# A Toeplitz and scan stage whose entries PE spreads into PSUM, with eight resident tiles selected late

## The reference, cut to what matters

```python
xn = (x - mu) / jnp.sqrt(var + LN_EPS) * ln_gamma + ln_beta   # x itself is layer-normed before
dA = jnp.exp(-jnp.exp(log_A) * dt[:, None]); dB = B_param * dt[:, None]
h = dA * h + dB * u[..., None]                                 # for each time step
y = einsum('dn,bdn->bd', C_param, h) + D_param * u
...
x = x + (residual + y @ W_out.T + b_out)
x = x + attention(ctx, ctx, layernorm(x)) @ W_out.T + b_out    # 64 keys, 16 heads
x = x + gated_ternary_ffn(layernorm(x))                        # 256 -> 1024 -> 1024 -> 1024 -> 256
```

## Time and profile before

| | |
|---|---|
| median of 3 runs | 933.9 us (932.27 to 935.5) |
| the profiled execution | 934.08 us, its span 932.3 us |
| PE busy | 869.6 us, 93% of the span |
| DVE, ACT, POOL busy | 514.6, 493.6, 183.2 us |
| chain that ended last | PE 89%, DVE 5%, issue 4%, ACT 1% |
| DMA | 61.79 MB; queue q8 for instructions: 24 packets, 0.39 MB |
| 20.0 to 51.4 us | PE busy 6.6, DVE 30.5, ACT 23.1, POOL 18.1; DMA share 0.96, 261 GB/s |
| 51.4 to 101.2 us | PE busy 44.1, DVE 36.9, ACT 28.7, POOL 36.4; granted clock 0.91 |
| 101.2 to 167.0 us | PE busy 58.3, DMA share 0.87 |

### The profile page before, as it was taken

One profiled execution on the slowest core, in us unless ns is written; L12 is line 12 of the kernel. 1 busy time (PEld: TensorE's weight loads), 2 busy tenths in 40 slices (PEclk: granted clock), 3 DMA queues, 4 the chain that ended last, 5 costly groups with the idle time before them and its releaser, 6 DMA issues.

```text
span 932.3 us, 15096 instructions
## 1 busy us (share of the span) xinstructions
PE 869.6 (93%) x5570; PEld 697.0 (75%) x5570; DVE 514.6 (55%) x927; ACT 493.6 (53%) x761; POOL 183.2 (20%) x201
## 2 busy tenths in 40 slices
PE   1168999899999999999999999999999999999997
PEld 0068867677777778777877887778778777777886
DVE  7987485465446464555555555554555456553411
ACT  2927533476356735764475536653575366635432
POOL 1567800500041002200230014000500050003000
PEclk9679999999999999999999999999999999999999
DMA  9961797500110002000200010001100110001000
GB/s 340 243 162 55 261 387 306 226 1 1 52 45 0 0 22 73 0 0 15 81 0 0 0 73 22 0 0 51 45 0 0 51 45 0 0 23 45 1 1 25
DMA packets 15497, 61.79 MB, mean 66 GB/s; under 512 B 2835, under 2 KB 4502, under 8 KB 14646
## 3 DMA queue, kind: packets, MB, share of 16 engines
q1 hardware_dynamic: 15430, 61.31, 19.0%
q0 software_dynamic: 32, 0.00, 0.0%
HBM read 49.63 MB, written 23.20 MB: 78 GB/s over the span
## 4 chain that ended last, share of the span: by engine, by line
PE 89%; DVE 5%; issue 4%; ACT 1%; POOL 0%; DMA 0%; SPq 0%; DVEq 0%; POOLq 0%
PE pair L1342 51%; PE pair L1329 11%; PE pair L1354 6%; PE pair L1269 4%; PE pair L1280 3%; PE pair L1296 3%; PE pair L470 2%; PE pair L477 2%; PE pair L1289 1%; PE pair L1319 1%; PE pair L1236 1%; PE pair L484 1%; PE pair L539 1%; DVE GG L337 1%; DVE stn L343 1%
## 5 line engine op out<-in xcount | busy, mean ns | idle before, releaser
L950 ACT ACTIVATE vbuf<-pair,scl 128x512 f32<-128x512 f32 x128 | 87.8, 686 | 231.0 <-PE pair L1342 222.1
L1342 PE MATMUL pair<-h2hi,h_turned 128*128 128x512 f32 x512 | 202.6, 396 | 0.0
L1342 PE MATMUL pair<-h2lo,h_turned 128*128 128x512 f32 x512 | 199.6, 390 | 0.0
L1342 PE MATMUL pair<-h1hi,h_turned 128*128 128x512 f32 x384 | 153.1, 399 | 0.0
L1342 PE MATMUL pair<-h1lo,h_turned 128*128 128x512 f32 x384 | 150.0, 391 | 0.0
L1118 DVE TENSOR_TENSOR h1lo<-vbuf,h1hi 128x512 fp32r<-128x512 f32 x80 | 57.7, 722 | 120.1 <-ACT h1hi L951 119.3
L1342 PEld LDWEIGHTS pair<-h2hi,h_turned 128*128 128x128 f32 x512 | 96.2, 188 | 25.2 <-issue 5.9
L1342 PEld LDWEIGHTS pair<-h2lo,h_turned 128*128 128x128 f32 x512 | 96.2, 188 | 19.3
L1118 DVE TENSOR_TENSOR h2lo<-vbuf,h2hi 128x512 fp32r<-128x512 f32 x64 | 44.2, 691 | 107.2 <-ACT h2hi L951 107.1
L1329 PE MATMUL pair<-zThi,w_turned 128*128 128x512 f32 x224 | 92.0, 411 | 2.9 <-DVE vbuf L1142 2.9
L1142 DVE SCALAR_TENSOR_TENSOR vbuf<-pair,scl,sg 128x512 f32<-128x512 f32 x64 | 47.9, 750 | 80.5 <-ACT sg L939 60.8
(11 more groups left out here) (145 smaller groups left out, 1593.3 us busy)
## 6 DMA issues: line engine op xcount, KB each, us to landing
h_turned<-d_h SPq DMA_DIRECT2D x2, 4096.0 KB, 15.1
xres<-in_x SPq DMA_DIRECT2D x8, 512.0 KB, 7.5
tok<-in_xs SPq DMA_DIRECT2D x8, 512.0 KB, 12.2
EE<-alpha_rows SPq DMA_DIRECT2D x16, 256.0 KB, 10.7
ring<-kernel_rows SPq DMA_DIRECT2D x16, 256.0 KB, 4.3
xr<-x_rows SPq DMA_DIRECT2D x8, 512.0 KB, 3.5
out<-xr SPq DMA_DIRECT2D x16, 256.0 KB, 2.1
x_rows<-xres SPq DMA_DIRECT2D x7, 512.0 KB, 12.4
```

The lines of the kernel that those rows point to most:

```text
L950: e.activation(vb[:, s % 2, :], h_ps[s % 4], ACT.Gelu, scale=sc)
L1342: ins = e.matmul(bank, w[:, k, m * P:(m + 1) * P], src[part][:, k, :], start=(k == 0 and part == 0), stop=(k == HC - 1 and part == 1))
```

## The change

It has these parts.

1. Entries. The store to `alpha_rows` and the sixteen entry loads are gone. PE spreads the exponents: for each channel a 64 x 64 matmul whose stationary operand is one column of the identity, broadcast to 64 columns, writes the exponent row to 64 partitions of PSUM. `spread_entries(n)` does groups n and n + 4 (64 matmuls), four times. ACT's `entry_exp` reads PSUM (`pair[STAGE[g]]`) and writes `EE`.
2. Row sums. All four column blocks accumulate in one PSUM pair with a shifted `pick` matrix in place of `ones`, so that two evacuations do instead of eight; the eight stores to DRAM remain. ACT's evacuation stands inside its norms, ahead of the fourth one (`ROWS_AT`).
3. Tiles. Eight resident Toeplitz tiles in place of the ring of four: four where the ring was, four where the weights w1 and w2 come later. All sixteen tile loads are issued at once in `sync_mixer`. All eight selects stand in `gpsimd_core`, after the third gamma.
4. Statistics. Eight of the 32 tile statistics (tiles 8 to 15) go from DVE to ACT (`tile_stats`: a Copy and a Square pass with summed output).
5. Small work. The D edits of `GG` and their undoing go from DVE to GpSimd and ACT; the PSUM clear of the state banks goes from DVE to five PE matmuls; ACT does 18 instead of 20 of each 32 norms; the loads of w1, w2, w3 to SBUF also wait for the last within.

```diff
+STAGE = {0: 3, 4: 0, 1: 2, 5: 1, 2: 3, 3: 2, 6: 0, 7: 3}
+EXP_AT = {g: n + 1 for n, g in enumerate(STAGE)}
-ACT_SHARE = 20
+ACT_SHARE = 18
+ACT_STATS = (8, 16)
+ROWS_AT = 3
+PAD = L
...
     def sync_mixer(e):
...
-        e.wait_ge(coef, 2)
-        for u in range(2):
-            e.dma_start(alS[P * (1 - u):P * (2 - u), :], al2[:, u, :]).then_inc(al_st, 16)
...
-        e.wait_ge(al_st, 32)
-        for g in range(2):
-            entries_load(e, g)
         e.dma_start(bo[:, :], a["ab"].partition_broadcast(P)).then_inc(wo_in, 16)
         e.dma_start(woT[:, :, :], a["aW"]).then_inc(wo_in, 16)
-        for v in range(4):
-            for h in range(2):
-                u = 2 * v + h
-                e.wait_ge(k_ev, u + 1)
-                c = (1 - h) * (P * L) + v * 2048
-                e.dma_start(kr[0, c:c + 2048].rearrange("(q m) -> q m", q=4), ksb[0:P:32, u, :]).then_inc(kr_st, 16)
-        for n in ("xW", "keys", "scl"):
-            e.dma_start(t[n], a[n]).then_inc(k_in, 16)
+        for h in range(2):
+            e.wait_ge(k_ev, h + 1)
+            for v in range(4):
+                c = (P * (1 - h) + 32 * v) * PAD
+                e.dma_start(kr[0, c:c + 32 * PAD].rearrange("(q c m) -> q c m", q=4, c=8)[:, :, 0:L],
+                            ksb[v:P:32, h, :].rearrange("q (c m) -> q c m", c=8)).then_inc(kr_st, 16)
         e.wait_ge(kr_st, 128)
         e.wait_ge(kr_pad, 16)
         for g in range(4):
             tt_load(e, g)
-        for g in range(2, NGRP):
-            entries_load(e, g)
+        for g in range(4, NGRP):
+            if g == 6:
+                e.wait_ge(nat_v, 1)
+            tt_load(e, g)
+        for n in ("xW", "keys", "scl"):
+            e.dma_start(t[n], a[n]).then_inc(k_in, 16)
 
     def sync_core(e):
-        for g in range(4, NGRP):
-            e.wait_ge(w_ps, 2 * (g - 4) + 2)
-            tt_load(e, g)
         e.wait_ge(h_ps, NOCT)
...
     def gpsimd_prep(e):
...
-        mask(e, 0)
...
-        for g in range(1, 4):
-            mask(e, g)
-        e.wait_ge(t_mask, 8)
 
     def gpsimd_core(e):
         e.wait_ge(wo_in, 32)
-        done = 0
-        for g, until in ((4, 0), (5, 0), (6, 0), (7, 4), (None, TILES)):
...
+        e.wait_ge(z_h, 3)
+        for g in range(NGRP):
+            mask(e, g)
+        e.wait_ge(t_mask, 2 * NGRP)
+        for tile in range(TILES):
+            bias(e, tile)
...
+        def tile_stats(first, until):
+            here, n = slice(first, until), until - ACT_STATS[0]
+            e.wait_ge(xr_in[first // 4], 16)
+            if n > 4:
+                e.wait_ge(t_var, n - 4)
+            for j in range(first, until):
+                e.activation(junk[j % 4], xres[:, j, :], ACT.Copy, accum_out=tsum[:, 0, j:j + 1]).then_inc(t_sum, 1)
+            e.wait_ge(t_sum, n)
+            e.activation(tsum[:, 1, here], tsum[:, 0, here], ACT.Copy, scale=-1.0 / (16 * DM)).then_inc(t_mean, 1)
+            e.activation(mvn[:, here, 0], tsum[:, 0, here], ACT.Copy, scale=1.0 / DM).then_inc(t_mean, 1)
+            e.wait_ge(t_mean, n // 2)
+            for j in range(first, until):
+                e.activation(junk[j % 4], xres[:, j, :], ACT.Square, bias=tsum[:, 1, j:j + 1], scale=1.0 / 16, accum_out=mvn[:, j, 1:2]).then_inc(t_var, 1)
...
+                if c == ROWS_AT:
+                    row_evac()
...
-        for v in range(4):
-            row_evac(v)
-        e.wait_ge(const, 9)
+        e.wait_ge(const, 10)
+        tile_stats(8, 12)
+        for g in (0, 4):
+            entry_exp(g)
+        tile_stats(12, 16)
+        for g in (1, 5, 2):
+            entry_exp(g)
         norm_apply(0)
-        entry_exp(0)
         norm_apply(1)
-        for g in range(1, 3):
+        for g in (3, 6, 7):
             entry_exp(g)
...
     def tensor(e):
...
         e.wait_ge(g_row, 7)
-        e.wait_ge(d_add, 4)
+        def spread_entries(n):
+            for i in range(GRP):
+                for g, h, u in ((n, 0, 0), (n + 4, 1, 1), (n, 1, 0), (n + 4, 0, 1)):
+                    rows, c = slice(N * u, N * u + N), GRP * g + i
+                    ins = e.matmul(pair[STAGE[g]][L * h:L * h + L, N * i:N * i + N], ident[rows, c:c + 1].to_broadcast([N, L]), al2[rows, 1 - h, :], start=True, stop=True)
+            ins.then_inc(e_ps, 1)
+        spread_entries(0)
+        e.wait_ge(pk_done, 7)
+        e.wait_ge(w_row, 2)
+        spread_entries(1)
+        e.wait_ge(e_rdy, EXP_AT[4])
+        spread_entries(2)
+        e.wait_ge(d_add, 2)
+        e.wait_ge(e_rdy, EXP_AT[5])
         for v in range(4):
...
-                    ins = e.matmul(kps[v % 2][h][32 * q:32 * q + 32, :], ones[N * h:N * h + N, 0:32], GGf[N * h:N * h + N, c:c + 8 * L], start=True, stop=True)
+                    ins = e.matmul(kps[h][32 * q:32 * q + 32, :], pick[N * h:N * h + N, 3 - v:35 - v], GGf[N * h:N * h + N, c:c + 8 * L], start=(v == 0), stop=(v == 3))
+        ins.then_inc(k_ps, 1)
+        e.wait_ge(e_rdy, EXP_AT[2])
+        spread_entries(3)
+        e.wait_ge(k_ev, 2)
+        e.wait_ge(dec0, 1)
+        e.wait_ge(z_b, 2)
+        for k in range(5):
+            e.matmul(hps[k % 2].rearrange("p (a d) -> p a d", a=4), ident[:, :], dec[:, :, 0].unsqueeze(1).to_broadcast([P, 4, P]), start=True, stop=True)
```

More of the change, by code:

```diff
@@ L79, in mixer_parts @@
     rev = sb("rev", [P, P], "c")
-    ones = sb("ones", [P, 32], "c")
+    pick = sb("pick", [P, 35], "c")
     stn = sb("stn", [P, TILES, 6], "d")
@@ L220, in gpsimd_prep @@
         e.memset(rev[:, :], 0.0).then_inc(const, 1)
-        e.memset(ones[:, :], 1.0).then_inc(const, 1)
+        e.memset(pick[:, :], 0.0).then_inc(const, 1)
         e.memset(mhalf[:, :], -0.5).then_inc(const, 1)
@@ L240, in gpsimd_prep @@
             e.tensor_tensor(rn[:, 0, here], sv[:, here], mhalf[:, 0:SB], ALU.pow).then_inc(powd, 1)
-        mask(e, 0)
-        e.wait_ge(t_mask, 2)
+        e.wait_ge(d_in, 32)
+        e.wait_ge(w_row, 2)
+        e.wait_ge(g_row, 7)
+        for row in (0, N):
+            v = GG[row:row + 1, :, L - 1]
+            e.tensor_tensor(v, v, edit[row:row + 1, 0, :], ALU.add).then_inc(d_add, 1)
+        e.wait_ge(d_add, 2)
+        power(0)
+        e.wait_ge(k_ps, 1)
+        e.wait_ge(powd, 1)
+        for row in (0, N):
+            e.tensor_copy(GG[row:row + 1, :, L - 1], edit[row:row + 1, 1, :]).then_inc(g_back, 1)
+        e.wait_ge(g_back, 2)
+        power(1)
         e.wait_ge(nat_v, 1)
+        e.wait_ge(powd, 2)
         e.tensor_tensor(rsm[:, :], svn[:, :], mhalf[:, :], ALU.pow).then_inc(natural, 1)
         e.wait_ge(natural, 1)
-        for g in range(1, 4):
-            mask(e, g)
-        e.wait_ge(t_mask, 8)
     def gpsimd_core(e):
         e.wait_ge(wo_in, 32)
-        done = 0
-        for g, until in ((4, 0), (5, 0), (6, 0), (7, 4), (None, TILES)):
[L254 to L260, removed]
+        e.wait_ge(z_h, 3)
[4 more added lines that the diff above has]
+            bias(e, tile)
     def scalar(e):
@@ L389, in vector @@
         double(4)
-        stats(4, 8)
+        stats(4, ACT_STATS[0])
+        last_two(0)
         double(5)
[L392 to L398, removed]
         variances(0)
-        stats(16, 26)
+        stats(SB, SB + 8)
         spreads(0)
-        stats(26, 32)
+        stats(SB + 8, TILES)
+        last_two(1)
         variances(1)
         e.tensor_scalar(svn[:, :], mvn[:, :, 1], EPS, None, ALU.add).then_inc(nat_v, 1)
-        for k in range(2):
-            e.memset(hps[k], 0.0).then_inc(h_zero, 1)
         norms(0)
         spreads(1)
-        e.wait_ge(k_ps, 4)
-        for row in (0, N):
-            e.tensor_copy(GG[row:row + 1, :, L - 1], edit[row:row + 1, 1, :]).then_inc(g_row, 1)
-        e.memset(dec[:, :, 0], 0.0).then_inc(dec0, 1)
         e.wait_ge(bc_in, 64)
         gamma(0)
-        norms(1)
         beta(0)
@@ L418, in vector @@
         beta(1)
+        norms(1)
         gamma(2)
@@ L476, in within @@
                 rows = slice(L * h, L * h + L)
-                ins = e.matmul(yps[o % 4][rows, c * BC:(c + 1) * BC], TT[o // 2 % 4][rows, (i % GRP) * L:(i % GRP + 1) * L], tok[rows, :, i], start=(c == 0), stop=False)
+                ins = e.matmul(yps[o % 4][rows, c * BC:(c + 1) * BC], TT[o // 2 % 8][rows, (i % GRP) * PAD:(i % GRP) * PAD + L], tok[rows, :, i], start=(c == 0), stop=False)
             return ins
@@ L500, in tensor @@
                 e.wait_ge(h_scan, o)
+            if o == 0:
+                e.wait_ge(e_rdy, EXP_AT[3])
             if o == 1:
-                e.wait_ge(g_row, 9)
+                e.wait_ge(g_back, 2)
+            if o == 2:
+                e.wait_ge(e_rdy, EXP_AT[6])
             if 4 <= o < NOCT:
```

109 lines of the change are left out of this document (58 added, 51 removed).

## The result

The changed kernel takes 944.1 us (median of 4 runs, 942.12 to 946.28) where the kernel before takes 934.3 us (4 runs, 932.27 to 935.5): ratio 1.0108, 95% interval 1.0074 to 1.0142, slower by 9.8 us. The forecast was 949, the range 936 to 957. The profiled execution took 942.32 us, its span 940.6.

The account below looks back on a forecast made before the run. The scan stage's end (102.4 us before) was taken to decide: turn 0 at 72.9 behind vblk + 43.5 stage + 1.4 contention = 117.8, 15.4 later; 934 + 15 = 949 us, range 936 to 957 (8 in 10).

Parts of the forecast that it names:

- The step that decides: Ahead of the scan stage: first select waits for vblk behind all tile loads; vblk at 69.8 us, turn 0 at 72.9.
- 44.9: Scan stage from turn 0 to its end: 43.5 us without state and stalls, plus 1.4 for contention.
- the row sums: PE's chain ahead of the tile loads: 6.59 us plus 1.5 for a falling clock, done at 40.3 (bounds 38.8 and 45.4).
- the 45 to 49 that I had named as the sign of being right: SP's queue: time in us of the first tile load in the new profile if the forecast holds.
- 117.8: Forecast end of the scan stage in us, against 102.4 before, 15.4 us later.
- rival D: Chain ahead of stage longer still: half-clock rows (+5.1), late instructions in new matmuls, table loads 2.6; up to 957, within 0.70.
- The 5.55 us of stalls: Old scan stage: PE stands still three times inside a turn, read as late instructions; booked as gone from the new stage.
- Contention: Scan stage: selects beside DVE's gammas and betas give a 3.5 us beat for six turns; 1.4 us booked (bounds 0 and 5.3).
- Rival A: vblk does not wait for the tiles; selects start when gamma(2) ends, turn 0 at 60.7, 937 us; chance 0.12.
- Rival B: Tile loads alone move at 414 GB/s: vblk at 62.1, turn 0 at 65.2, 942 us; chance 0.09.
- Rival C: Stage wins: row sums ready at 35.9 so ACT never stands, vblk as in A; end 98.9, 930.5 us; chance 0.09.
- C's threshold of 56.1: Scan stage: turn 0 must start by 56.1 us for the kernel to be faster by over 0.3% (2.8 us).

Follow-up runs that it names:

- The two kernels that give A what it assumed: Changed kernel with the vblk load issued ahead of stores and tile loads: 936.76 us; changed kernel with GpSimd's vblk clears moved behind its selects and biases: 936.63 us.
- the early-spread kernel: Changed kernel with the vblk load first and the wait for the six doublings moved from the first entry matmuls to the row sums: 928.65 us.
- the last expectation: For the early-spread kernel with norms four entries later, zeroing matmuls cut from five to two: 923 to 925 us expected, 928.85 measured.

## Why the prediction was right, and where its sizes were off

**The step that decides held.** The select waits for vblk, vblk waits for everything ahead of it in the queue: foreseen from 46.70 + 12.7 in the old trace, and shown by four kernels from both sides (load first, clear last, load after six groups, and the old kernel with its selects moved). From the first tile load to the landing I had 22.5 us; it took 65.1 - 41.36 = 23.7. Turn 0 came 3.1 after the landing, as I had it. From turn 0 to the stage's end I had 44.9; it took 44.0.

**The mis-sized term: the row sums.** I gave them the 6.59 us of the earlier trace rows and 1.5 for a clock that falls. They took 3.66. The 64 matmuls had run at a mean of 993 ns before and 592 after, so the row I priced from was itself a slow one, though the granted clock of that stretch reads 1.00. Nor did PE stand idle ahead of them: the spread ran until they began. That makes 4.4 us. ACT's statistics were also shorter (4.1, not 5.0, with no table load), so that the row sums began 0.7 earlier, and from their end to the first tile load it took 6.2 us instead of 7.0. So the first tile load was issued at 41.36 instead of 47.3, outside the 45 to 49 that I had named as the sign of being right; of these 5.9 us, 1.2 went back to the queue, and 0.9 came off the stage. That is the whole of 117.8 against 112.3. The pause of PE in the new matmuls (2.16 us), which I had in rival D alone, cost nothing, because ACT was busy with the statistics; the kernel with statistics on DVE shows that it does cost when that cover is gone.

**Pauses gone.** The 5.55 us of stalls of the old stage are gone in the changed kernel, as booked, and the cause I could only suggest is now shown: a copy that nothing waits for makes new ones, and every pause of 0.5 us or more ends just after an instruction packet has landed. When the tiles load under the stage again they return in part only, 2.4 and 3.3 us in all. Why pauses of 0.3 to 0.7 us come without DMA traffic in some executions is open.

**Contention.** I booked 1.4 of a beat of 3.5 us for six turns; the trace has 3.28 for four. The Trainium skill, "SBUF — State Buffer", section "SBUF: two separate sides", has VectorE and GpSimd exclude each other for a whole instruction, whichever starts first; the trace agrees. My 2.35 would hold only for a gamma that starts together with a select. The gammas and betas of 2.10 start 0.1 us behind one, wait for its end and then end 1.07 to 1.08 later; where the beta came first, the select waited. So 2.15 in the old row was no sign against the rule, as I had read it.

**Rival A** (vblk does not wait) did not happen by itself: 64 KB needed 10.4 to 11.5 us. The Trainium skill, "DMA: Bandwidth & Descriptors", part "HWDGE ordering", allows a later load to complete first where it uses fewer engines; here vblk landed at 65.1, with the DMA share down to 0.05 from 64 us on. The two kernels that give A what it assumed land at 936.8 and 936.6, and A's price was 937. It came out by luck, by two errors that cancel: turn 0 was at 57.5 and 57.1, not 60.7, and the stage took 48.3 and 46.4 from there, not 44.9. **Rival B** fell: 230 GB/s, not 414. **Rival C**'s part was right: ACT stood only 0.62 us for the rows, not until 40.3. With vblk out of the way turn 0 was at 57.1, one microsecond from C's threshold of 56.1, but the end was 46.4 later and not 43.5. C's sum had assumed a stage without stalls and without contention; the kernel with vblk cleared last has 2.4 us of pauses in it, and DVE's gammas and betas beside selects. Even the changed kernel, whose turn 0 waits until the tiles have landed, took 44.0. Of **rival D** one part came, the pause in the new matmuls, and it cost nothing; the rest did not.

## What to carry to other kernels

Moving work to another place in an in-order program moves it behind every wait that stands there: a clear of one small buffer, harmless for 0.2 us, became the gate of the whole stage and cost 7.4 of the 9.8 us; the other 2.4 are the longer chain ahead of the stage, and spreading the entries early took them back and more. Check, for each moved block, the last wait ahead of it on its engine, and all bytes ahead of that transfer in its queue. And before a chain is shortened, ask what the next limit is: here a start 5.1 us earlier gained nothing, because PE then ran under the loads it no longer waited for, and its instructions came late. Take a duration from a row only after asking at what rate that row ran. And a piece called "issue" in a chain of waits is a pause of PE only if PE's own timeline has it: in the kernel with vblk loaded first the chain has 1.41 us of "issue" at 59.64, while DVE was running a beta of 1.94 us.

## What the runs showed of the hardware that was not expected

- Matmuls of one shape took 993 ns (before) and 592 ns (after) on average; in the first case PE had been idle for 14.6 us, and the granted clock in the row reads 1.00 from 20.4 to 27 us and 0.68 from 27 to 35. Single ones take about 590 or about 1058 ns; in the early-spread kernel the median is 1057 where the column reads 0.50, and before it is 1057 where the column reads 1.00. So a duration can be a truer witness of the clock than its column.
- In all eleven kernels that spread entries PE's first pause by "issue" comes after exactly 220 records of the spread (1.78 to 3.27 us), in the changed kernel with 406 GB/s of DMA traffic beside those records. With 350 GB/s of copy traffic ahead of it and 300 beside it a pause in the turns lasted 4.24 us.
- A pass of ACT with summed output is followed by an instruction of its own that reads the sum, 0.18 to 0.20 us, about half of it hidden under the pass: eight passes and two small ones in 4.1 us.
- Ten 128x512 records (five matmuls) that clear PSUM took 8.9 us, four took 3.75, and in the changed kernel the granted clock beside the ten reads 0.50 until 51 us and 1.00 from 52 on without a change in their pace. So, as far as that column can be trusted, "half the clock" in the last expectation is not what made them slow; what does is open. Six fewer moved state(0) by 2.9 us.
